# A recurrent step by two prefix scans: the candidate and the new state, each from four interleaved operands

## The reference

```python
def step(h, xt):
    xr_t, xz_t, xn_t = xt
    r = jax.nn.sigmoid(xr_t + h @ w_hr.T + b_hr)
    z = jax.nn.sigmoid(xz_t + h @ w_hz.T + b_hz)
    n = jnp.tanh(xn_t + r * (h @ w_hn.T + b_hn))
    h_new = (1.0 - z) * n + z * h
    return (h_new, h_new)
```

## Time and profile before

| | |
|---|---|
| median of 3 runs | 1646.24 us (1638.33 to 1646.63) |
| span of the profiled execution | 1636.9 us |
| TensorE busy | 1365.0 us (83%) |
| VectorE busy | 1143.2 us (70%) |
| ScalarE busy | 704.4 us (43%) |
| GpSimd busy | 434.8 us (27%) |

### The profile page before, as it was taken

How to read it: one execution, slowest core, us unless ns; L and a number is a source line. 1 busy time by engine, 2 the same in 40 slices (tenths; PEclk the granted TensorE clock), 3 DMA queues, 4 the chain that set the end, 5 groups by cost and what they waited for, 6 DMA issues and landing times. The chain is left out here.

```text
span 1636.9 us, 65673 instructions
## 1 busy us (share of the span) xinstructions
PE 1365.0 (83%) x27355; PEld 1027.9 (63%) x27370; DVE 1143.2 (70%) x5594; ACT 704.4 (43%) x2475; POOL 434.8 (27%) x818
## 2 busy tenths in 40 slices
PE   5888888878878888888888887379999999999886
PEld 4667777767767777777777776245556555555443
DVE  5767777777777777777777776557576776776485
ACT  3333223222222222222222222136777777777765
POOL 2001111111111111111111111364245535522354
PEclk6555555555555555555555555578999999999998
DMA  5200000000000000000000000068537735742001
GB/s 120 29 4 5 5 7 5 5 6 5 5 5 7 5 5 6 5 5 7 5 5 7 5 5 7 7 140 139 73 66 110 98 58 89 106 68 29 1 14 39
DMA packets 68941, 53.70 MB, mean 33 GB/s; under 512 B 12686, under 2 KB 68390, under 8 KB 68646
## 3 DMA queue, kind: packets, MB, share of 16 engines
q1 hardware_dynamic: 66470, 49.32, 18.3%
q10 hardware_dynamic: 2176, 0.20, 0.1%
HBM read 31.84 MB, written 15.47 MB: 29 GB/s over the span
## 5 line engine op out<-in xcount | busy, mean ns | idle before, releaser
L731 PE MATMUL PS<-GB,W 128*128 128x8 f16 x18432 | 575.7, 168 | 177.3 <-DVE GB L1041 173.2
L731 PEld LDWEIGHTS PS<-GB,W 128*128 128x128 f16 x18432 | 532.6, 104 | 285.9 <-DVE GB L1041 281.1
L935 ACT ACTIVATE tr<-PS 128x16 f32<-128x16 f32 x512 | 94.7, 185 | 490.2 <-PE PS L731 490.2
L2383 DVE TENSOR_REDUCE MX<-PS 128x1 f32<-128x512 f32 (+3 forms) x352 | 220.0, 635 | 114.8 <-PE PS L1842 111.6
L2121 ACT ACTIVATE PT<-PS 128x512 f32<-128x512 f32 (+1 forms) x352 | 193.2, 566 | 114.7 <-PE PS L1858 110.1
L937 ACT ACTIVATE tz<-PS 128x16 f32<-128x16 f32 x512 | 94.2, 184 | 192.0 <-PE PS L731 192.0
L1027 DVE SCALAR_TENSOR_TENSOR u_<-tr,PS 128x16 f32<-128x16 f32 x512 | 87.4, 171 | 126.0 <-PE PS L731 114.0
L685 POOL TENSOR_TENSOR rt<-mv,eps 128x1 f32<-128x1 f32 x96 | 18.4, 191 | 553.1 <-DVE mv L1052 553.1
L1034 DVE SCALAR_TENSOR_TENSOR zg<-tz,HR 128x16 f32<-128x16 f32 x512 | 90.1, 176 | 81.5 <-ACT tz L937 81.4
L1839 PE MATMUL PS<-KS,QS 99*128 99x256 bf16 (+3 forms) x512 | 134.0, 314 | 12.8 <-DVE MX L2383 8.5
L1855 PE MATMUL PS<-QS,KS 102*128 102x256 bf16 (+3 forms) x512 | 128.8, 302 | 6.2 <-ACT PT L2121 5.6
(11 more groups left out here) (393 smaller groups left out, 2496.8 us busy)
## 6 DMA issues: line engine op xcount, KB each, us to landing
QS<-q_parts SPq DMA_DIRECT2D x90, 128.0 KB, 11.0
KS<-k_parts SPq DMA_DIRECT2D x90, 128.0 KB, 13.1
q_parts<-PQ SPq DMA_DIRECT2D x16, 384.0 KB, 10.4
k_parts<-PK SPq DMA_DIRECT2D x16, 384.0 KB, 3.3
X<-XM SPq DMA_DIRECT2D x32, 64.0 KB
out_dram<-X SPq DMA_DIRECT2D x8, 256.0 KB, 2.3
XM<-in_L_attn_x_dram SPq DMA_DIRECT2D x16, 80.0 KB
s_hh<-in_L_attn_w_hh_dram SPq DMA_DIRECT2D x1, 768.0 KB, 5.4
```

The source lines that it names most:

```text
L731: return pe.matmul(bank[:, p, at:at + B], W[:, kc, w:w + P], state[:, part, kc, :], start=False, stop=True, skip_group_check=True)
L935: act.activation(as_states(tr), now(pR), ACT.Tanh, scale=gate_scale).then_inc(hn_tr.sem, 1)
L2383: dve.tensor_reduce(MX[:, g % 2, heads[0]:heads[-1] + 1, NT - 1 - it], p_x[:, k % 2, 0:len(heads) * w].rearrange("p (a w) -> p a w", w=w), ...
```

## The change

The two sums of products of a step are each computed by one prefix scan. A scan goes along its operands with s = a s + b, and gives out every s. Four operands are interleaved for each of the 16 numbers of a state, so that a scan is 64 wide, and the first factor of each four is 0, which cuts it off from the four before.

- Candidate: factors `RQ` = (0, 1, tr, 1), of which only tr is written in a step (ACT, every fourth float). The summands lie in PSUM: (product with the low state, product with the high state, low product + input, high product). The fourth result is (1 + tr) x product + input, as `v_` was.
- State: factors `ZQ` = (0, 1, tz, -1), of which tz is written by ACT; summands `NQ` = (-h/2, n, -h/2, n), where h is the kernel's state. ACT's tanh writes n twice, at a step of two floats. The scan runs twice, into `GQ` (16 bits, fourth result the high state) and into `HR` (floats). The low state is written into the third place of `GQ`, and -h/2 of the new state into `NQ` (a new VectorE instruction).

`RQ` and `ZQ` are filled once at the start. TensorE reads the states from `GQ`, at every fourth 16-bit place. The candidate's products with W1 take the high and the low state in one product of 32 columns (4 a step, for 8), and those with W2 write two places of PSUM each (16 columns, 4 a step). So a step has 32 products instead of 36: 8 of r and 4 of the candidate ahead of the wait for the low state, 4 of r, 4 of the candidate, 12 of z. Biases and inputs of the candidate are put into every second or fourth place of PSUM. Since `GQ` is overwritten in each step, ACT copies high and low into `GB` for the projection (`keep`), between the tanhs of r and z.

The diff, cut to the step:

```diff
@@ TensorE
-                    for w in by_g1[:3]:
-                        product("n", p, k, state, *w, 0)
+                    for w in tiles:
+                        candidate_w2(p, k, state, *w)
                     pe.wait_ge(g2_ready.sem, n)
-                    for w in by_g2:
-                        last = product("r", p, k, state, *w, 1)
+                    for w in tiles:
+                        last = product("r", p, k, state, *w, W1, LOW)
                     last.then_inc(r_ps.sem, 1)
-                    for w in by_g1[3:]:
-                        product("n", p, k, state, *w, 0)
-                    for w in by_g2:
-                        last = product("n", p, k, state, *w, 1)
+                    for w in tiles:
+                        last = candidate_w1(p, k, state, *w)
                     last.then_inc(hn_tr.sem, 1)
+                def candidate_w2(p, k, state, mc, kc):
+                    w = (HC * 2 + mc) * P
+                    return pe.matmul(candidate(p)[:, k, mc, :, 1:4:2], W2[:, kc, w:w + P],
+                                     state[:, kc, :, HIGH].unsqueeze(2).to_broadcast([P, B, 2]),
+                                     start=False, stop=True, skip_group_check=True)
+                def candidate_w1(p, k, state, mc, kc):
+                    w = (HC * 2 + mc) * P
+                    return pe.matmul(candidate(p)[:, k, mc, :, :].rearrange("p b (o i) -> p b o i", o=2), W1[:, kc, w:w + P],
+                                     state[:, kc, :, LOW:HIGH + 1].unsqueeze(2).to_broadcast([P, B, 2, 2]),
+                                     start=False, stop=True, skip_group_check=True)
@@ ScalarE
+                def keep(n, ring, s):
+                    act.wait_ge(g2_ready.sem, n + 1)
+                    act.activation(GB[:, ring, :, :, s, :].rearrange("p i c b -> p c b i"), GQ[:, :, :, LOW:HIGH + 1],
+                                   ACT.Copy).then_inc(states_kept.sem, 1)
-                    act.activation(as_states(tr), now(pR), ACT.Tanh, scale=gate_scale).then_inc(hn_tr.sem, 1)
+                    act.activation(third(RQ), now(pR), ACT.Tanh, scale=gate_scale).then_inc(hn_tr.sem, 1)
+                    if not (isinstance(first, int) and first + s == 0):
+                        keep(first + s, *((ring, s - 1) if s else ((ring - 1) % RG, GS - 1)))
...
-                    act.activation(n_[:, :], v_[:, :], ACT.Tanh, scale=n_scale).then_inc(n_ready.sem, 1)
+                    act.activation(NQ[:, :, 1:4:2], v_[:, :, 3:4].to_broadcast([P, NSTEP, 2]), ACT.Tanh, scale=n_scale).then_inc(n_ready.sem, 1)
@@ VectorE
-                    dve.scalar_tensor_tensor(by_chunk(u_[:, :]), by_chunk(tr[:, :]), 1.0, hn,
-                                             ALU.add, ALU.mult).then_inc(u_ready.sem, 1)
-                    dve.wait_ge(u_ready.sem, n)
-                    dve.tensor_tensor(by_chunk(v_[:, :]), by_chunk(u_[:, :]), xn, ALU.add).then_inc(v_ready.sem, 1)
+                    dve.tensor_tensor_scan(one_row(v_[:, :, :]), one_row(RQ[:, :, :]), hn_and_xn, 0.0,
+                                           ALU.mult, ALU.add).then_inc(v_ready.sem, 1)
...
-                    dve.scalar_tensor_tensor(high, by_chunk(zg[:, :]), 0.5, by_chunk(zn[:, :]), ALU.mult, ALU.subtract).then_inc(g1_ready.sem, 1)
-                    dve.scalar_tensor_tensor(now, zg[:, :], 0.5, zn[:, :], ALU.mult, ALU.subtract).then_inc(g_ready.sem, 1)
+                    dve.tensor_tensor_scan(GQ[:, :, :, :].rearrange("p c b i -> p (c b i)"), one_row(ZQ[:, :, :]), one_row(NQ[:, :, :]), 0.0,
+                                           ALU.mult, ALU.add).then_inc(g1_ready.sem, 1)
+                    dve.tensor_tensor_scan(one_row(HR[:, :, :]), one_row(ZQ[:, :, :]), one_row(NQ[:, :, :]), 0.0,
+                                           ALU.mult, ALU.add).then_inc(g_ready.sem, 1)
                     dve.wait_ge(g_ready.sem, n)
-                    dve.tensor_tensor(low, by_chunk(now), high, ALU.subtract).then_inc(g2_ready.sem, 1)
+                    dve.tensor_tensor(GQ[:, :, :, LOW], by_chunk(HR[:, :, 3]), GQ[:, :, :, HIGH], ALU.subtract).then_inc(g2_ready.sem, 1)
+                    dve.tensor_scalar(NQ[:, :, 0:3:2], HR[:, :, 3:4].to_broadcast([P, NSTEP, 2]), -0.5, None, ALU.mult).then_inc(half_ready.sem, 1)
```

More of the change, by code:

```diff
@@ L471, in build, with candidate @@
             pN = PS[:, 4:6, :]
+            def candidate(p):
+                return pN[:, p, 0:4 * U * NSTEP].rearrange("p (u c b i) -> p u c b i", u=U, c=HC, i=4)
             hr_start = signal("hr_start")
@@ L724, in _ @@
                 by_g1 = [(mc, kc, W) for mc in range(HC) for kc in range(HC) for W in (W1, W2)]
-                by_g2 = [(mc, kc, W1) for mc in range(HC) for kc in range(HC)]
+                tiles = [(mc, kc) for mc in range(HC) for kc in range(HC)]
                 def product(gate, p, k, state, mc, kc, W, part):
@@ L730, in product @@
                     at = (mc * U + k) * B
-                    return pe.matmul(bank[:, p, at:at + B], W[:, kc, w:w + P], state[:, part, kc, :],
+                    return pe.matmul(bank[:, p, at:at + B], W[:, kc, w:w + P], state[:, kc, :, part],
+                                     start=False, stop=True, skip_group_check=True)
[8 more added lines that the diff above has]
+                                     state[:, kc, :, LOW:HIGH + 1].unsqueeze(2).to_broadcast([P, B, 2, 2]),
                                      start=False, stop=True, skip_group_check=True)
                 def inject(gates_at, p, rows, start):
-                    for bank, first, bias, chunk in gates_at:
+                    for bank, which, bias, chunk in gates_at:
                         for mc in range(HC):
-                            o = bank[:, p, first + mc * U * B:first + (mc + 1) * U * B]
+                            if which is None:
+                                o = bank[:, p, mc * U * B:(mc + 1) * U * B]
+                            else:
+                                o = candidate(p)[:, :, mc, :, which].rearrange("p u b i -> p u (b i)")
                             if bias is not None:
-                                pe.matmul(o, brow[:, (bias + mc) * P:(bias + mc + 1) * P], ones3[:, :],
+                                n = 2 * U * B if which == HIGHS else U * B
+                                pe.matmul(o, brow[:, (bias + mc) * P:(bias + mc + 1) * P],
+                                          ones3[:, 0:n] if which is None else ones3[:, 0:n].rearrange("p (u n) -> p u n", u=U),
                                           start=start and mc == 0, stop=False, skip_group_check=True)
@@ L802, in early @@
                         for h, w in TERMS:
-                            last = pe.matmul(p_gy, GB[:, ring, h, c, :, :].rearrange("p t b -> p (t b)"), OU[w][:, c, :],
+                            last = pe.matmul(p_gy, GB[:, ring, 1 - h, c, :, :].rearrange("p t b -> p (t b)"), OU[w][:, c, :],
                                              start=(c == 0 and h == 0 and w == 0), stop=(c == 1 and h == 1), skip_group_check=True)
@@ L932, in steps @@
                     now = lambda bank: bank[:, p, 0:U * NSTEP].rearrange("p (c u b) -> p c u b", c=HC, u=U)[:, :, k, :]
[L933 removed]
+                    third = lambda x: x[:, :, 2].rearrange("p (c b) -> p c b", c=HC)
+                    if isinstance(first, int) and first == 0 and s == 0:
+                        act.wait_ge(hr_start.sem, 6)
                     act.wait_ge(r_ps.sem, n)
[L935 removed]
+                    act.activation(third(RQ), now(pR), ACT.Tanh, scale=gate_scale).then_inc(hn_tr.sem, 1)
+                    if not (isinstance(first, int) and first + s == 0):
+                        keep(first + s, *((ring, s - 1) if s else ((ring - 1) % RG, GS - 1)))
                     act.wait_ge(z_ps.sem, n)
[L937 removed]
+                    act.activation(third(ZQ), now(pZ), ACT.Tanh, scale=gate_scale).then_inc(tz_ready.sem, 1)
                     act.wait_ge(v_ready.sem, n)
[L939 removed]
+                    act.activation(NQ[:, :, 1:4:2], v_[:, :, 3:4].to_broadcast([P, NSTEP, 2]), ACT.Tanh, scale=n_scale).then_inc(n_ready.sem, 1)
+                    if isinstance(first, int) and first + s == S - 1:
+                        keep(S, ring, s)
                 def inputs(j, s):
@@ L1021, in steps @@
                     by_chunk = lambda x: x.rearrange("p (c b) -> p c b", c=HC)
-                    hn, xn = [pN[:, p, i * U * NSTEP:(i + 1) * U * NSTEP].rearrange("p (c u b) -> p c u b", c=HC, u=U)[:, :, k, :]
-                              for i in range(2)]
-                    before, now = HR[:, 1 - s % 2, :], HR[:, s % 2, :]
+                    one_row = lambda x: x.rearrange("p n i -> p (n i)")
+                    hn_and_xn = candidate(p)[:, k, :, :, :].rearrange("p c b i -> p (c b i)")
@@ L1033, in steps @@
+                    if not (isinstance(first, int) and first == 0 and s == 0):
```

(3 more changed lines are left out.)

63 lines of the change are left out of this document (33 added, 30 removed).

## The result

The changed kernel takes 1666.34 us (median of 4 runs, 1662.18 to 1672.15) against 1646.43 for the kernel before on the same chip (1638.33 to 1648.63). The ratio is 1.0129, with a 95% interval of 1.0097 to 1.016: the change makes the kernel slower by 20 us. The forecast was 1619, so its direction was wrong.

A forecast was written before the change was run, and what follows sets the result against it. One ring of dependencies, 1.94 us a step, was taken as the bound; new links 1.05 + 0.22 + 0.32 + 0.26 + 0.04 = 1.89 save 27 us, net 25 after overruns: 1619 us, forecast 1605 to 1635, range 1580 to 1667.

The forecast's parts named there:

- the sum: The recurrence step's links added up: 1.89 us against 1.94, 0.05 a step less, 512 times, 27 us.
- Tanh of n to state scan: Link of a recurrence step from n's tanh on ACT to the state scan's start, forecast at 0.26 us.
- the ring: The closed chain of dependent instructions through one recurrence step, whose links add up to 1.94 us before the change.
- full-rate: Rival: a scan keeps the rate of other vector instructions, 0.215 us; 1.69 us a step, 1518 us; chance 0.06.
- dear scan: Rival: a scan costs more than twice the rate; at 0.33 us the step is 2.02, 1687 us; chance 0.04.
- The ring through both state scans and the low part: Link from state scan to tanh of r: TensorE waits 0.08 us for the low part; 1.05 us in all.
- The two slots: Other work in a step, N1 with the sum behind it and MAX8, given 0.59 us of room.
- overruns: Slots of other work that exceed their room by 0.03 us, for which 2 us were added in total.
- the fourth rival: W2 matmuls writing every second PSUM place are slow; at eight times their places, 0.11 us each, 1750 us; chance 0.04.
- The first rival: Strided results cost in all three links, 0.15 us instead of 0.04; step 2.00, 1676 us; chance 0.12.

The follow-up runs named there:

- the kernel of 1619.5 us: The changed kernel with the state scan's three waits written in another order, n, half, tz instead of half, tz, n: 1619.5 us, ratio 0.9849 to the kernel before.

## Why the prediction was wrong

**The step that failed.** It is the sentence "The state scan names three semaphores, of which n's comes last; behind it stand HR's scan and low, already in the sum, and the halving." The listing ahead of the prediction showed the three waits, the forecast named them and asked what stands behind the waiting instruction, but it gave the wait itself the price of a single one. The term that is too small is "Tanh of n to state scan", 0.26. In the kernel before no wait that ends last on the ring has company, so no row of the forecast showed a price; the cost was not bounded, as an unseen one should have been. It measures 0.098 a step (0.362 against 0.264), 50 us: more than the 27 that the rest of the sum gains.

Off the ring the trace of the kernel before does hold the price. L2477, in the third stage, has three waits in 6 of its 24 executions, and the one that ends last there, for a result of VectorE itself, stands in a sequencer's instruction ahead of it. Counted from that semaphore's update, the instruction starts 0.129 later; zn, with its one wait, starts 0.024 behind the update that it waits for, and the state scan of the changed kernel 0.121. So the term could have been bounded before the run.

**What the sum had right.** With that one wait mended, by either way, the kernel takes 1619.5 and 1620.9 us where 1619 was forecast, and a step 1.888 and 1.887 where 1.89 was. That it fits so closely is in part luck: 0.02 too little up to r's tanh and 0.03 too much behind it cancel. By its terms:
- The scan: 287 ns for the candidate, as taken, neither 0.215 nor 0.52. The Trainium skill (DVE: opcode table, instruction layouts, handler registers and perf-mode slots; section Datapath and trigger behaviour) says half throughput; the 287 ns agree, at two times 1.04 ns an element on top of a 16-wide instruction. All scans here are 64 wide, so the price of an element is not measured by itself. The duration refutes the full-rate and the dear scan.
- The ring through both state scans and the low part: 1.069 to r's tanh, for 1.05. TensorE waits: its 13th product starts 0.098 behind the 12th, at a pitch of 0.027 otherwise, a wait of 0.07 where 0.08 was given; then it loses 0.020 behind the first product after the wait, which the sum did not have.
- Candidate: the scan is released by r's tanh and not by TensorE, 0.230 behind its start; z's tanh ends before n's.
- The two slots: the mean step lies 0.006 above the median (1.989, 1.983), before 0.003; that is 1.5 us more, for the 2 given to overruns.

**What it sized wrongly, at little cost.** r's strided tanh takes 198 ns instead of 185, 0.013 for the 0.04 charged. The low part takes 196 instead of 175 ns (0.02, given as nothing), so it pays more than r, where the forecast had r alone pay; it also reads at every fourth place now, and no run separates the two. n's takes 232 for 229, the copy 337 for 230, hidden as forecast. The W2 products, at every second place of PSUM, keep the pitch of 0.027, so the fourth rival falls; at twice their places they would keep it too, so a cost of up to that is not excluded. The input products do not all stay as they were (columns as in the earlier trace rows):

```profile
L763 PE MATMUL PS<-Y,V x2322: 187/188/242, 23.4 to 1042.1; 128*128 128x32 f16 x194
```

Two thirds (1548) take 188 ns as before, the others 214 to 242: they are the six that stand in a row in every fourth step, whose 32 outputs now stand at every fourth place. They start 0.053 apart, where the same six were 0.027 apart before. They lie behind z's last product, off the ring. The Trainium skill (PSUM — Partial Sum Buffer, section Specifications) has any non-contiguous pattern slow matmuls significantly; these 0.053 us agree, the 16 outputs at every second place do not show it.

**The rivals.** The measured 1666 lies just inside the stated range of 1580 to 1667 by luck: its upper end was set by rivals of another kind. The first rival (all strided results dear, 1676) gave a time close to the measured one, but not its mechanism: n and low stayed at 232 and 196 ns, below the 245 and 200 at which it was to begin, and the same strided results stand in the kernel of 1619.5 us. No rival had the wait. A rival of the kind "the new join of three releases costs more than one" would have been its place.

**Where the expected gain went.** It is there, and it is the candidate's: from r's tanh to n's a step of the changed kernel takes 0.552 instead of 0.650, 0.098 less. The state's half takes some 0.04 back by way of the low part, and its waits another 0.098; from 1.940 that leads to 1.98. The halves measured alone (0.057 won, 0.04 lost) do not add up to the two together with one wait (0.053 won). Alone, the candidate's half pays 0.025 for the 12th product ahead of the wait; beside the two scans that product costs nothing, since TensorE waits for the low part anyway (first product to r's tanh 0.719 with 12 ahead, 0.721 with 11). The candidate's half with 11 products ahead of the wait wins 0.081 and is faster, at 1606 us, than the whole change with its waits mended, at 1620.

## What to carry to other kernels

Where an instruction waits for several semaphores, look which of them it carries itself and which go to the sequencer ahead of it: in these runs the wait that ends last must be the one written first, or all must raise one semaphore. Fusing two 16-wide instructions into one 64-wide scan paid here for u_ and v_, and lost for zn and high, where the low part queued behind a second scan: look at what is needed soon behind the fused instruction, and test the halves of a change apart, and together. Where two branches end together, count the products ahead of the wait: one of 0.027 us was some 10 us here.

## What was not expected of the hardware

- A sequencer's wait that ends last: 0.130 from the release to the start of the instruction, against 0.032 for a wait carried by the instruction; nothing if it ends earlier (1.888 against 1.887 a step).
- A granted clock that TensorE's own records do not bear out. For the recurrence the profile of the kernel with n's wait first gives a granted clock of 1.00 (2.4 GHz), that of the kernel with one semaphore 0.50 (1.2 GHz). The stretch from 100 to 900 us, of the former and of the latter: its length, busy us and count of PE, PEld (weight loads), DVE, ACT and POOL, then the granted clock, DMA's share and GB/s:

```profile
100.00:900.00 800.00, 697.21 (x17329) 604.05 (x17326) 573.37 (x2885) 363.55 (x1803) 130.87 (x310) 1.00 0.02 5
```

```profile
100.00:900.00 800.00, 697.99 (x17359) 604.96 (x17356) 574.19 (x2893) 362.84 (x1805) 130.32 (x310) 0.50 0.02 5
```

  Products of 128 columns of 16-bit numbers tell the two levels apart, but not these two runs. In that stretch they take 314 ns in the former and in the latter, and where two such products stand next to each other, the second starts 0.106 behind the first in both (median):

```profile
L872 PE MATMUL PS<-DN,IL 128*128 128x128 f16 x104 | 32.7, 314 | 0.0
```

```profile
L870 PE MATMUL PS<-DN,IL 128*128 128x128 f16 x104 | 32.7, 314 | 0.0
```

  From 1250 to 1400 us, where both profiles give 1.00, such products take some 220 ns and start 0.055 apart; of the former:

```profile
L1870 PE MATMUL PS<-maskU,identb 128*128 128x128 bf16 x163 | 27.6, 219 | 0.0
```

  So the equal pitch (0.027), step (1.888 and 1.887) and time (1619.5 and 1620.9) of the two do not show that the clock is without effect here. What a higher clock would do to the recurrence, and why the one row reads 1.00, stay open.
